# Second attention: scores as one product over 96 stacked rows, output product in plain single precision, and some waits moved in the first attention

## The reference

```python
def _L0_xattn_ref(...):      # 32 heads of 128, masked, with position bias
    score = jnp.einsum('bqhd,bkhd->bhqk', h_q, h_k)
    score = score + position_bias[None]
    score = jax.nn.softmax(jnp.where(m, score, -jnp.inf), axis=-1)
    attn = jnp.einsum('bhqk,bkhd->bqhd', score, h_v).reshape(b, lq, H * DH)
    return hidden_states + attn @ w_out.T

def _L1_xattn_ref(queries, keys, values, Wq, Wk, Wv, Wo):   # 8 key heads, 4 query heads on each, 16 wide
    q = (queries @ Wq).reshape(b, s, KV_HEADS, GROUP, HEAD_DIM)
    k = (keys @ Wk).reshape(b, s, KV_HEADS, HEAD_DIM)
    v = (values @ Wv).reshape(b, s, KV_HEADS, HEAD_DIM)
    scores = jnp.einsum('bqhgd,bkhd->bhgqk', q, k) * scale
    attn = jax.nn.softmax(scores, axis=-1)
    out = jnp.einsum('bhgqk,bkhd->bqhgd', attn, v)
    return out.reshape(b, s, EMBED) @ Wo

x = x + _L0_xattn_ref(_layernorm(x), ctx, ...)
x = x + _L0_ffn_ref(_layernorm(x), ...)
x = x + _L1_xattn_ref(_layernorm(x), ctx, ctx, ...)
x = x + _L1_ffn_ref(_layernorm(x), ...)      # layers 2 and 3 follow
```

## Time and profile before

| | us |
|---|---|
| median of 3 runs | 1857.78 |
| their range | 1857.41 to 1859.46 |
| the profiled execution's own time | 1858.16 |
| its span | 1856.2 |

### The profile page before, as it was taken

One profiled execution on the slowest core, in us unless ns is written; L12 is line 12 of the kernel. 1 busy time (PEld: TensorE's weight loads), 2 busy tenths in 40 slices (PEclk: granted clock), 3 DMA queues, 4 the chain that ended last, 5 costly groups with the idle time before them and its releaser, 6 DMA issues. The chain is left out here.

```text
span 1856.2 us, 29556 instructions
## 1 busy us (share of the span) xinstructions
PE 1786.5 (96%) x10312; PEld 1504.4 (81%) x10312; DVE 1414.3 (76%) x2854; ACT 650.3 (35%) x1783; POOL 672.8 (36%) x453
## 2 busy tenths in 40 slices
PE   8999999999999999997998998879999999999998
PEld 6888889889988889986875665675888888888886
DVE  7767777777777777776546867879788888888886
ACT  5432232123333223224025765530343433343333
POOL 6643343444443333332150003434443333243331
PEclk9999999999999999999999998989999999999999
DMA  4111101111111110111010002010111110111011
GB/s 173 62 51 51 51 23 49 36 45 51 51 51 51 51 48 24 34 40 59 2 46 20 1 26 69 24 64 1 46 35 35 34 35 33 34 34 36 32 35 46
DMA packets 32026, 78.27 MB, mean 42 GB/s; under 512 B 4096, under 2 KB 10944, under 8 KB 31584
## 3 DMA queue, kind: packets, MB, share of 16 engines
q1 hardware_dynamic: 31968, 77.50, 12.8%
HBM read 75.39 MB, written 2.10 MB: 42 GB/s over the span
## 5 line engine op out<-in xcount | busy, mean ns | idle before, releaser
L658 POOL TENSOR_TENSOR l0x_comb<-l0x_neg,l0x_bias 128x1024 f32<-128x1024 bf16 x32 | 69.0, 2155 | 371.8 <-DVE l0x_probs L1056 358.5
L950 ACT ACTIVATE l0x_probs_t<-bank 128x512 f32<-128x512 f32 x32 | 19.1, 597 | 500.6 <-PE bank L795 500.6
L2910 POOL TENSOR_TENSOR l3x_q<-l3x_q,l3x_cross 128x512 f32<-128x512 f32 x64 | 89.8, 1407 | 187.9 <-DVE l3x_q L1881 187.9
L39 PE MATMUL bank<-l0x_w_v_hi,ctx_lo 128*128 128x256 f32 x512 | 144.9, 283 | 0.0
L37 PE MATMUL bank<-l0x_w_v_hi,ctx_hi 128*128 128x256 f32 x512 | 144.9, 283 | 0.0
L38 PE MATMUL bank<-l0x_w_v_lo,ctx_hi 128*128 128x256 f32 x512 | 144.9, 283 | 0.0
L934 ACT ACTIVATE l0x_probs<-l0x_probs,l0x_top 128x129 f32<-128x129 f32 x256 | 99.4, 390 | 53.3 <-DVE l0x_top L1060 53.3
L3097 ACT ACTIVATE l3x_probs<-l3x_probs,l3x_top 128x128 f32<-128x128 f32 x256 | 99.1, 389 | 38.1 <-DVE l3x_top L3178 38.0
L37 PE MATMUL bank<-ctx_hi,l0x_w_k_hi 128*128 128x512 f32 x256 | 104.0, 406 | 7.7 <-DVE ctx_lo L1138 7.7
L1100 DVE TENSOR_TENSOR x<-x,bank 128x512 f32<-128x512 f32 x120 | 82.1, 684 | 37.4 <-PE bank L39 37.4
L37 PE MATMUL bank<-l3x_qin_hi,l3x_w_q_hi 128*128 128x512 f32 x256 | 105.2, 411 | 2.2 <-ACT l3x_v L3131 1.9
(11 more groups left out here) (488 smaller groups left out, 5330.4 us busy)
## 6 DMA issues: line engine op xcount, KB each, us to landing
l0x_raw_k<-L_k_dram SPq DMA_DIRECT2D x32, 256.0 KB, 3.4
l0x_raw_v<-L_v_dram SPq DMA_DIRECT2D x16, 512.0 KB, 3.3
l0x_raw_q<-L_q_dram SPq DMA_DIRECT2D x16, 512.0 KB, 4.3
l0x_raw_o<-L_o_dram SPq DMA_DIRECT2D x16, 512.0 KB, 3.4
l3x_raw<-L_q_dram SPq DMA_DIRECT2D x16, 512.0 KB, 3.3
l3x_raw<-L_o_dram SPq DMA_DIRECT2D x16, 512.0 KB, 3.3
kv_raw<-L_kv_dram SPq DMA_DIRECT2D x8, 512.0 KB, 3.4
l0x_ctx_raw<-ctx_t_dram SPq DMA_DIRECT2D x4, 512.0 KB, 5.3
```

Of the source, the lines that this page charges most:

```text
L39: return pe.matmul(out, lhs[1], rhs[0], start=False, stop=stop)
L658: pool.tensor_tensor(comb[:, :, :], neg[:, :, :], bias[:, j:j + 1, :].to_broadcast([P, B, P]), ALU.add).then_inc(comb_ready, 1)
L950: act.activation(probs_t[:, 0:BH, :], bank[6][:, :].rearrange("p (b n) -> p b n", b=BH), ACT.Copy).then_inc(t_act, 1)
L2910: pool.tensor_tensor(dst[:, part], dst[:, part], cross[n][:, :], ALU.add).then_inc(rotated, 1)
```

## The change

**Layer 0.** PE's `scores` waits for the first drained half before its first four products and for both before the next four; in all periods but the first these were drained long before. In the last step ACT makes the high part of head 30, before its exponentials of head 31, in place of DVE's two CASTs. DVE's `copy_probs` goes between the adds and the maximum of `add_bias(LAST)`, and the last ranking round with L1130 goes behind the normalisation.

**Layer 1.** Keys: `kd` is one tensor of four quads with zeros but for the head's own rows. POOL zeroes three quads behind `rstd` and DVE the fourth behind `xn`; when both are done and both halves of `kt` are split, 24 SP DMAs of 16 rows x 1024 columns fill it. POOL's four products and its `select` table are gone. Queries: `stack` holds high, low and high part in 96 rows, filled by SP DMAs of 32 rows: for batch 0, 12 for each group, each group behind the landing of the one before; then 12 for each batch, from batch 2 on behind the scores of batch b - 2. Scores: four products of 96 rows and 256 columns for a unit. Output product: `w_o` is loaded as it is and used in plain single precision, 4 products of 512 columns (8 records) for a batch; ACT copies `at` once, into one of two buffers, and DVE's `result_low` is gone. `ffn.load` moves to before batch 4's queries. `query_high(1, g)` and `query_low(1, g)` are placed one unit later for g over 0.

```diff
-                def scores(h, j, needed):
-                    pe.wait_ge(ring_drained, needed)
+                def scores(h, j, first_half, both):
                     wait(pe, scores_read, 2 * h)
                     for half in range(2):
+                        pe.wait_ge(ring_drained, both if half else first_half)
...
-                    scores(h, 0, 8 if first else at(p - 1, "k_even1") + 1)
+                    if first:
+                        scores(h, 0, 7, 8)
+                    else:
+                        scores(h, 0, at(p - 1, "k_even1") + 1, at(p - 1, "k_even1") + 1)
...
                     copy_probs(h)
+                    if last:
+                        heads_high(h, 0)
                     exps(h + 1, 1)
...
+                    if ahead_of_top:
+                        ahead_of_top()
...
-                            rank_round(p - 1, 3 + m)
-                        rank_end(p - 1)
+                            if m < 3 or not last:
+                                rank_round(p - 1, 3 + m)
+                        if not last:
+                            rank_end(p - 1)
...
-                    add_bias(LAST, 1)
-                    copy_probs(LAST - 1)
-                    for half in range(2):
-                        dve.wait_ge(h_full, 2 * (LAST - 1) + half + 1)
-                        dve.tensor_copy(heads[0][:, 0, half * HALF:(half + 1) * HALF], bank[6 + half][:, :]
-                                        ).then_inc(h_hi, 1)
+                    add_bias(LAST, 1, lambda: copy_probs(LAST - 1))
                     heads_low(LAST - 1, 0)
                     normalise(LAST, 1)
+                    rank_round(N - 2, ROUNDS)
+                    rank_end(N - 2)
                     copy_probs(LAST)
                     heads_low(LAST, 1)
...
+    QUADS, ROWS, PARTS, KEY_PARTS = 4, 32, (0, 1, 0), (0, 0, 1)
+    STACK = ROWS * len(PARTS)
+    LANDED = 16 * QUADS * len(PARTS)
...
-        kd = pair("kd", [P, BH, T])
-        w_o = pair("w_o", [P, G, D])
+        kd = sb("kd", [P, QUADS, 2, T], F32R)
+        w_o = sb("w_o", [P, G, D])
+        stack = [sb("stack0", [P, G, QUADS, P], F32R), core.stack_kept]
...
-                sp.wait_ge(w_ready, 1)
-                sp.wait_ge(raw_loaded, 16)
-                sp.dma_start(raw[:, :, :], dram["L1x_wo"]).then_inc(raw_loaded, 16)
-                sp.wait_ge(q_full, 2 * G)
-                sp.wait_ge(w_ready, 2)
-                ffn.load(sp)
+                sp.wait_ge(kd_zero, 2)
+                sp.wait_ge(kt_done, 2)
+                for s, part in enumerate(KEY_PARTS):
+                    for j in range(QUADS):
+                        for m in range(2):
+                            head = slice(j * ROWS + m * HD, j * ROWS + (m + 1) * HD)
+                            sp.dma_start(as_f32(kd[s * ROWS + m * HD:s * ROWS + (m + 1) * HD, j, m, :]),
+                                         as_f32(kt[part][head, :])
+                                         ).then_inc(kd_done, 16)
+                sp.dma_start(w_o[:, :, :], dram["L1x_wo"]).then_inc(wo_loaded, 16)
+
+                def stack_queries(b, units):
+                    for s, part in enumerate(PARTS):
+                        for j in range(QUADS):
+                            sp.dma_start(as_f32(stack[b % 2][s * ROWS:(s + 1) * ROWS, units, j, :]),
+                                         as_f32(q[part][j * ROWS:(j + 1) * ROWS, units, b * P:(b + 1) * P])
+                                         ).then_inc(stacked[b % 2], 16)
+
+                for g in range(G):
+                    sp.wait_ge(q_done, g + 1)
+                    wait(sp, stacked[0], LANDED * g)
+                    stack_queries(0, slice(g, g + 1))
+                sp.wait_ge(vt_full, 2)
+                stack_queries(1, slice(0, G))
+                for b in range(2, B):
+                    if b == BH:
+                        sp.wait_ge(q_done, 2 * G)
+                        sp.wait_ge(w_ready, 1)
+                        ffn.load(sp)
+                    sp.wait_ge(s_full, G * (b - 1))
+                    stack_queries(b, slice(0, G))
...
+                pool.memset(as_f32(kd[:, 0:QUADS - 1, :, :]), 0.0).then_inc(kd_zero, 1)
...
-                pool.wait_ge(select_ready, 1)
-                for half in range(2):
-                    pool.wait_ge(kt_done, half + 1)
-                    for s in range(2):
-                        pool.tensor_tensor(kd[s][:, :, half_of(half)],
-                                           as_f32(kt[s][:, half_of(half)]).rearrange("p (o k) -> p o k", o=1)
-                                           .to_broadcast([P, BH, HALF]),
-                                           select[:, :].rearrange("p (s o) -> p s o", o=1).to_broadcast([P, BH, HALF]),
-                                           ALU.mult).then_inc(kd_done, 1)
-                split_low(1, w_o)
...
-                    for n, (ql, kl) in enumerate(((0, 0), (1, 0), (0, 1))):
-                        for r in range(ROW_TILES):
-                            rows = slice(r * ROWS, (r + 1) * ROWS)
-                            mm = pe.matmul(bank[2 * (u % 2) + r][:, :].rearrange("p (m k) -> p m k", m=BH),
-                                           q[ql][rows, g, tokens], kd[kl][rows, :, tokens], start=n == 0, stop=n == 2)
+                    if b == 0:
+                        pe.wait_ge(stacked[0], LANDED * (g + 1))
+                    elif g == 0:
+                        pe.wait_ge(stacked[b % 2], LANDED * (b // 2 + (G if b % 2 == 0 else 1)))
+                    for j in range(QUADS):
+                        mm = pe.matmul(bank[2 * (u % 2) + j // 2][:, j % 2 * 2 * P:(j % 2 + 1) * 2 * P]
+                                       .rearrange("p (m k) -> p m k", m=2), stack[b % 2][0:STACK, g, j, :],
+                                       kd[0:STACK, j, :, tokens], start=True, stop=True)
...
-                        mm = product(pe, bank[7][:, :], [at[s][:, g, :] for s in range(2)],
-                                     [w_o[s][:, g, :] for s in range(2)], g == 0, g == G - 1)
+                        mm = product(pe, bank[7][:, :], [at[:, b % 2, g, :]], [w_o[:, g, :]], g == 0, g == G - 1)
...
-                pe.wait_ge(kd_done, 2)
+                pe.wait_ge(kd_done, 2 * LANDED)
...
-                        pe.wait_ge(kd_done, 4)
-                        pe.wait_ge(w_ready, 2)
+                        pe.wait_ge(wo_loaded, 16)
...
-                def result_high(b):
+                def copy_result(b):
                     act.wait_ge(at_full, b + 1)
-                    wait(act, o_full, b)
-                    act.activation(at[0][:, :, :], bank[6][:, :].rearrange("p (g t) -> p g t", g=G), ACT.Copy
-                                   ).then_inc(at_hi, 1)
+                    wait(act, o_full, b - 1)
+                    act.activation(at[:, b % 2, :, :], bank[6][:, :].rearrange("p (g t) -> p g t", g=G), ACT.Copy
+                                   ).then_inc(at_done, 1)
...
+                    if u == 0:
+                        query_high(1, 0)
+                    if 2 <= u <= G:
+                        query_high(1, u - 1)
                     if u >= 1:
                         copy_probs(u - 1)
-                    if u < G:
-                        query_high(1, u)
                     if u >= 6 and (u - 6) % G == 0:
-                        result_high((u - 6) // G)
...
+                dve.memset(as_f32(kd[:, QUADS - 1, :, :]), 0.0).then_inc(kd_zero, 1)
...
-                def result_low(b):
-                    dve.wait_ge(at_hi, b + 1)
-                    dve.tensor_tensor(at[1][:, :, :], bank[6][:, :].rearrange("p (g t) -> p g t", g=G),
-                                      as_f32(at[0][:, :, :]), ALU.subtract).then_inc(at_done, 1)
```

More of the change, by code:

```diff
@@ L86, in keep_kv @@
     def keep_kv(self, ctx):
-        self.sb(ctx, "l1_wkv_kept", [P, 2, DC * 2 * P])
+        self.stack_kept = self.sb(ctx, "l1x_stack1", [P, 4, 4, P], F32R)
     def statistics(self, dve, b):
@@ L861, in period @@
                         project_out(p - 1, at(p, "out"))
-                    scores(h + 1, 1, at(p, "k_odd") + 2)
+                    scores(h + 1, 1, at(p, "k_odd") + 1, at(p, "k_odd") + 2)
                     transpose_probs(h, 0)
@@ L1048, in _, with add_bias @@
             def _(dve):
-                def add_bias(h, j):
+                def add_bias(h, j, ahead_of_top=None):
                     dve.wait_ge(comb_ready, h + 1)
@@ L1317, in l1_layer @@
     KV, G, HD = L1_GROUPS, L1_QUERIES, L1_DIM
-    ROWS, COLS = 64, 32
-    ROW_TILES, COL_TILES = P // ROWS, P // COLS
+    COLS, COL_TILES = 32, 4
+    QUADS, ROWS, PARTS, KEY_PARTS = 4, 32, (0, 1, 0), (0, 0, 1)
+    STACK = ROWS * len(PARTS)
+    LANDED = 16 * QUADS * len(PARTS)
     UNITS = B * G
@@ L1341, in l1_layer @@
         ot, inv = sb("ot", [P, 2, G, P]), sb("inv", [P, G * KV])
-        a, at = sb("a", [P, G, KV, HD]), pair("at", [P, G, P])
```

(27 more changed lines are left out.)

4 lines of the change are left out of this document (3 added, 1 removed).

## The result

The changed kernel takes 1881.43 us, median of four runs (1880.52 to 1882.94), against 1858.04 (1857.41 to 1859.46) of the kernel before in the same comparison: 23.4 us slower, a ratio of 1.0124 with a 95% interval of 1.0108 to 1.0140. The forecast was 1875.0, 16.8 slower, in a range of 1860 to 1884.

What follows compares the result with a forecast made beforehand. It took PE's work to bound most of layer 0, waits its last step and layer 1's opening, a DVE-ACT circuit layer 1's batches; -1.3 - 4.8 + 20.3 + 1.0 + 0.8 + 0.8 = +16.8 on 1858.16 gave 1875.0, range 1860 to 1884.

Steps and rivals of the forecast that it cites:

- the opening: Layer 1's start up to the first reciprocal: memsets and SP's DMA issues delay it from 1006.74 to 1027.0, +20.3 us.
- SP's queue: Layer 1's opening: 81 DMA issue steps (40.5 us) and four landings (8.3 us) behind `kt_lo`, all on the path.
- Layer 0, first period: PE's waits for a drain before its first and second scores shrink: 0.79 to 1.57 us gained, taken as -1.3.
- Layer 0, last step: End of layer 0: earlier adds and projection let the last copy start at 844.0 to 845.3, not 849.44; taken as -4.8.
- The block: Layer 1's opening: POOL's instructions hold DVE's `xn`, so `kt_lo` ends at 965.7 instead of 954.07.
- the uncertain step: Layer 1's opening: that POOL's memset holds DVE, which no row showed; without it `kt_lo` ends at 954.1.
- the case with quick issues: Rival for layer 1's opening: POOL holds DVE, but DMA issues take 0.34 us; 81 steps cost 27.5, total 1862; chance 0.09.
- the circuit: Layer 1's batch loop through DVE and ACT: scores -0.6, output product +0.7, together +0.1 a batch; +0.8 in all.
- From unit 4 to the reciprocal: Layer 1's opening: from unit 4's start, units 4 and 5, last query and unit 6 onward take 12.4 us.
- the clock: Layer 1's opening: PE waits in short turns, so its clock may stay low; +1.0 us (0 to 3).
- The end: Layer 1's end: the last two output products come exposed after the last unit, each 0.35 dearer for a half; +0.8.

## Why the prediction was right

The direction, the mechanism and the range held. The middle was 6.4 us short of the median, and the terms show where; those in the opening are measured from the first `xn`. That the range held is in part luck, as the term of SP's queue was 10.7 us too small and others made up for it.

- **Layer 0, first period**: -1.3 forecast. The waits of the earlier trace rows went whole. DVE's add into x (L1100, in the changed kernel L1107) that stands at 831.89 stands at 830.11, 1.78 sooner; but 0.43 of that was there before the edited place. Counted from the eight records at 35.39 and 34.96 it is 1.35, and in the trace of layer 0's edits alone 1.40 (35.32 to 830.42). So this term was right.
- **Layer 0, last step**: -4.8 forecast in 3.5 to 5.9; 7.65 less 1.78 is 5.9, at the edge. At the ranking's new place L1137 took 0.29 us, where the earlier trace rows has 1.75 for it, and the last copy started at 841.77, over a microsecond sooner than the 843 to 844 that I had. Together the layer gave 7.65 in this trace, 7.3 in the medians, and not 6.1.
- **The block**: 19.1 us from the first `xn` to the end of `kt_lo` forecast, 17.8 measured. The size was right, its working was not: I let DVE through between every two of POOL's instructions, and the second `xn` stood through two of them. It cost nothing: six `xn` come behind POOL's third instruction either way, and POOL was through with its three 11.5 us after the first `xn`'s start, where I had 12.9. That a memset holds DVE, the uncertain step, is shown by two kernels, with `xn` and with `var_eps`. The rule of the Trainium skill ("SBUF — State Buffer", Who interferes with whom), an exclusive lock held for the whole instruction, agrees with these two.
- **SP's queue**: here the sum was short. The step was taken from `ffn.load` as 0.5 us; it is 0.63. 25 issues took 15.8 and not 12.6, the first group 8.8 and not 7.5, and the next four 35.0 and not 28.8: 10.7 us over 81 steps. The prediction set the ten DMAs of the earlier trace rows apart as ones that do not cross partitions, but that does not explain the step: `w_o` comes from HBM as they do, and its issue took 0.58 with the next one 0.63 behind it. Two of the ten themselves (`l1f_keys` at 993.35 and `l1f_values` at 993.98 in the trace of before) took 0.59 each and stand 0.63 apart; taking the mean hid them. The 0.34 of the case with quick issues was no step of theirs: their shortest issue took 0.33, but the next one came 0.38 behind it (991.89 and 992.27). What sets a step between 0.38 and 0.63 is open. The prediction named the issue time as what could make it wrong, and put steps of 0.6 with landings of 2.5 past 1884. The steps were 0.63, and the time stayed under 1884 because layer 0 came out 1.6 better, the block 1.3 and the circuit 1.7: without these it is 1886.
- **From unit 4 to the reciprocal**: 12.4 and 1.0 for the clock forecast, 13.8 measured; the two are not told apart.
- **The circuit**: +0.1 a batch forecast, -0.18 measured. It was the difference of two terms, -0.6 and +0.7, of which the runs show -0.85 and +0.65; so the scores' gain was the one that I had too small.
- **The end**: +1.0 forecast for the eighth batch and the last output products. The trace has 0.3 and 0.6, and 1.4 in stages that the change does not touch.

In one sum: layer 0 1.6 better than forecast, the opening 9.9 worse, the circuit 1.7 better, the end 1.4 worse, at least half of it this execution's own.

The estimate of 2.13 us for DVE's memset, from the one cycle an element that the Trainium skill has ("VectorE: DVE Perf Modes", Zero memsets can be issued as uint32 (trn2)), does not agree with the trace: it took 1.76, 0.86 ns an element. The measurement decides; it moved the sum by 0.3.

## What to carry to other kernels

Count DMAs on one queue as one counts instructions: at 0.63 us each, 12 small ones in a chain are a stage of their own, with 32 as with 64 KB, and here one DMA for four groups was worth more than a start after the first group. Before putting a long instruction on POOL, look at what DVE runs in the same stretch, not only at whether POOL is idle; and look at what keeps POOL idle, since a barrier cannot be used as spare time. An edit made of several parts can hide one good part: here 0.85 us a batch from the stacked scores was spent by 0.65 on the output product and by 31 us in the opening, and measured as a whole it was only slower. And before a difference of 2 or 3 us is read, look in the traces for a stretch that the edit does not touch: one in L1Ffn differed by up to 2.7 us.

## What the runs showed of the hardware

- A MEMSET on POOL holds a TENSOR_SCALAR on DVE: 5.43 us for one that takes about 0.5 alone, and 4.54 us for one of 0.17. The prediction's rows had shown it for a TENSOR_TENSOR on POOL only.
- It does not hold every instruction of DVE: a MEMSET of 2048 elements took 1.76 us beside POOL's memset, as without it, and two TENSOR_TENSOR from a bank 1.29, against 1.22.
- The second `xn` waited through two POOL instructions in a row (4.52 and 1.80 us). Which of two engines that wait comes first at such a boundary is not settled: the first `xn` got in after the first memset, the second did not get in between the next two.
- An issue of a DMA from partition to partition on SP takes 0.59 us and the next starts 0.63 after it; 32 or 64 KB make no difference, and the twelve of 16 KB in a group stand 7.6 us in all, 0.63 each, too. Ten issues of loads from HBM stood 0.51 apart in the mean, 0.53 in the changed kernel, but two of the ten stood 0.63 apart, and that of `w_o`, also from HBM, took 0.58 and the next came 0.63 later.
- The eight records of a plain product of 512 columns took 3.60 us in the changed kernel's end, and at full clock the products of 96 rows and 256 columns started 0.12 to 0.15 us apart, where two of 128 rows stand 0.12 apart.
- One stretch of L1Ffn, with the same work, took 18.6 us at a granted clock of 0.79 to 0.84 in seven profiled executions and 20.1 to 21.3 us at 0.74 to 0.76 in four.
